# Two heads' scan decays in one place of an image-pair cycle of a gated state-space block

## What is computed

```python
xz = silu(einsum('oc,bchw->bohw', in_proj_w, x) + in_proj_b)
x_ssm, res, gate = split(xz, 3, axis=1)
xf = silu(conv1d(x_ssm, dw_w) + dw_b)
dbc = einsum('oc,bcn->bon', dbc_w, xf) + dbc_b      # per head: dt, B (8 states), C (8 states)
x_h, dt, B_t, C_t = tokens in the order perm[h]       # gathered
dA = exp(softplus(dt) * -exp(A_log));  dB = dt * B_t
h = dA_t * h + dB_t * x_t;  y_t = sum_s h * C_t        # over 1024 tokens, 2 heads, 8 states
y = (y back in image order) * silu(gate) + res
x = x + silu(einsum('oc,bchw->bohw', out_proj_w, y) + out_proj_b)
```

## Time and profile before

| | |
|---|---|
| three runs | 837.87, 838.59 and 839.11 us (median 838.59) |
| the profiled execution | 842.28 us, span from first to last instruction 840.5 us |
| mean granted clock of TensorE | 0.939 of 2.4 GHz |
| busy share of the span | PE 88%, DVE 71%, ACT 61%, POOL 42% |
| chain that ended last | POOL 28%, PE 20%, DMA 19%, DVE 15%, issue 13%, ACT 4% |

### The profile page before, as it was taken

How to read it: one execution, slowest core, us unless ns; L and a number is a source line. 1 busy time by engine, 2 the same in 40 slices (tenths; PEclk the granted TensorE clock), 3 DMA queues, 4 the chain that set the end, 5 groups by cost and what they waited for, 6 DMA issues and landing times.

```text
span 840.5 us, 11680 instructions
## 1 busy us (share of the span) xinstructions
PE 735.4 (88%) x4190; PEld 435.9 (52%) x4190; DVE 592.7 (71%) x1097; ACT 508.6 (61%) x954; POOL 354.4 (42%) x325
## 2 busy tenths in 40 slices
PE   2599867929999999999999999999999999697976
PEld 1356556614566456545755565546654566354642
DVE  5699589624787578957894779577957786378533
ACT  5775745426764875488467756676667764544422
POOL 2295300377038711873087407760577037600330
PEclk9699857969999999999999999999999999998989
DMA  9924550248464937484747564765568434942332
GB/s 329 369 101 165 143 128 1 83 134 212 107 213 144 245 87 246 136 215 120 219 143 189 164 183 156 190 194 131 195 191 213 115 131 142 254 114 87 110 92 100
DMA packets 128539, 136.40 MB, mean 162 GB/s; under 512 B 57305, under 2 KB 107106, under 8 KB 126434
## 3 DMA queue, kind: packets, MB, share of 16 engines
q1 hardware_dynamic: 114448, 99.42, 41.3%
q0 software_dynamic: 12288, 35.80, 13.1%
q10 hardware_dynamic: 1746, 0.45, 0.3%
HBM read 83.08 MB, written 53.61 MB: 163 GB/s over the span
## 4 chain that ended last, share of the span: by engine, by line
POOL 28%; PE 20%; DMA 19%; DVE 15%; issue 13%; ACT 4%; SPq 0%; POOLq 0%; DVEq 0%; ACTq 0%
POOL xt_scratch L462 15%; POOL crow L476 11%; DMA out<-xb 7%; PE pj L1557 7%; PE pj L1429 5%; DMA xb<-in_x 3%; DMA crow<-yt_scratch,idx 3%; DMA xt_scratch<-stage,idx 3%; DVE xf L1040 2%; DVE rs L894 2%; PE tp L1547 2%; POOL xb L443 2%; DMA crow<-cd_scratch 1%; PE tp L1449 1%; DVE xb L1225 1%
## 5 line engine op out<-in xcount | busy, mean ns | idle before, releaser
L1429 PE MATMUL pj<-xb,inw 128*128 128x512 f32 x768 | 350.4, 608 | 21.5 <-POOL xb L443 16.0
L1429 PEld LDWEIGHTS pj<-xb,inw 128*128 128x128 f32 x768 | 144.7, 194 | 187.2 <-issue 155.9
L462 POOL DMA_INDIRECT xt_scratch<-stage,idx x128 | 152.0, 1188 | 80.9 <-issue 73.7
L476 POOL DMA_INDIRECT crow<-yt_scratch,idx x128 | 135.0, 1054 | 109.5 <-DMA yt_scratch<-rs 62.1
L443 POOL TENSOR_SCALAR xb<-xb,pcur 128x1024 f32<-128x1024 f32 x30 | 46.5, 1559 | 257.2 <-DMA xb<-in_x 170.3
L1040 DVE SCALAR_TENSOR_TENSOR xf<-xs,small,xf 128x1024 f32<-128x1024 f32 x64 | 83.9, 1322 | 76.0 <-ACT xf L634 74.5
L1557 PE MATMUL pj<-gt,outw 128*128 128x512 f32 x256 | 118.9, 596 | 0.1
L734 ACT ACTIVATE rs<-pj,small 128x512 f32<-128x512 f32 x64 | 44.2, 694 | 58.1 <-PE pj L1557 58.0
L677 ACT COPY stage<-tp 128x256 f32<-128x256 f32 x128 | 47.8, 374 | 44.9 <-PE tp L1451 42.1
L690 ACT COPY rs<-pj 128x512 f32<-128x512 f32 x64 | 33.0, 600 | 67.7 <-PE pj L1524 67.7
L703 ACT ACTIVATE gt<-pj,pcur 128x512 f32<-128x512 f32 x64 | 41.5, 687 | 46.0 <-PE pj L1429 45.9
(11 more groups left out here) (256 smaller groups left out, 1059.0 us busy)
## 6 DMA issues: line engine op xcount, KB each, us to landing
xb<-in_x SPq DMA_DIRECT2D x16, 1024.0 KB, 5.7
xp<-xt_scratch SPq DMA_DIRECT2D x16, 1024.0 KB, 9.6
crow<-cd_scratch SPq DMA_DIRECT2D x16, 1024.0 KB
out<-xb SPq DMA_DIRECT2D x16, 1024.0 KB, 6.4
yt_scratch<-rs SPq DMA_DIRECT2D x16, 512.0 KB, 3.6
yt_scratch<-rs SPq DMA_DIRECT2D x32, 256.0 KB, 5.4
gt<-in_x SPq DMA_DIRECT2D x4, 1024.0 KB, 12.0
big<-in_x SPq DMA_DIRECT2D x4, 1024.0 KB, 13.7
```

Of the source, the lines that this page charges most:

```text
L462: pool.indirect_dma_start(out=xt_d.ap(), out_offset=bass.IndirectOffsetOnAxis(ap=idx[:, k:k + 1], axis=0), in_=v(stage, (nt * H + h) * ROW ...
L476: pool.indirect_dma_start(out=v(crow, k * NB * P, (1, NB * P)), out_offset=None, in_=yt_d.ap()[0:(h + 1) * N], in_offset=bass.IndirectOffs ...
L1429: last = nc.tensor.matmul(o[:, :], v(inw, ct * 3 * C + col + ot * P, (1, P)), x_view(par, b, ct, nt * HALF, HALF), start=(ct == 0), stop=( ...
```

## The change

`big` now has room for both heads (2 x 8 x 272 columns in place of 8 x 272 and 8 x 256), and the token products are written over the decays they come from, not to a part of their own. ACT's `decays(i+1, 1)` follows `decays(i+1, 0)` directly, ahead of the output units of cycle `i`; `convolved(i+2, 1)` moves from ahead of the decays to behind output unit 3. PE's `segments(i+1, 1)` stands behind output unit 0, ahead of its tile of rows, and waits until head 0's decays are done (`ee_ready`), since `sg` holds one head. `turn_c(i+1, 0)` moves from ahead of unit 4 to ahead of unit 5 and waits for both heads' decays. In the setup, `segments(0, 1)` and `decays(0, 1)` come ahead of `turn_c(0, 0)` on PE and of `convolved(1, 1)` on ACT. On POOL, cycle 0 alone has its scatters ahead of both scalings; from cycle 1 on the order is the old one.

```diff
-        big = sb("big", S * EEW + S * Q * L)
+        big = sb("big", H * S * EEW)
...
             def cycle(i):
+                early = 1 if i else 0
                 if i < PH - 2:
-                    scale_x(i + 2, (0,))
+                    scale_x(i + 2, range(0, early))
                 if i < PH - 1:
                     scatter(i + 1)
                 if i < PH - 2:
-                    scale_x(i + 2, (1,))
+                    scale_x(i + 2, range(early, NB))
...
             def decays(i, h):
-                wait(act, w_ready, i * H + h)
+                wait(act, m_step, (i - 1) * H * 6 + (h + 1) * 6)
...
-                    last = nc.scalar.activation(v(big, s * EEW, (1, EEW)), v(sg, 0, (1, EEW)), ACT.Exp,
+                    last = nc.scalar.activation(v(big, h * HEAD + s * EEW, (1, EEW)), v(sg, 0, (1, EEW)), ACT.Exp,
...
                 if more:
                     rows_out(i + 1, 1)
-                if more:
-                    decays(i, 1)
-                    if not first(i):
-                        gate(i, par, range(0, 4))
-                else:
-                    gate(i, par, range(0, 2))
-                    decays(i, 1)
-                    gate(i, par, range(2, 4))
+                if not first(i):
+                    gate(i, par, range(0, 4))
...
                 residual(i, par, range(2, E_U))
-                if beyond:
-                    convolved(i + 2, 1)
                 if more:
-                    decays(i + 1, 0)
+                    for h in range(H):
+                        decays(i + 1, h)
                 for k in range(O_U):
                     output(i, (k,))
                     if beyond:
                         rows_out(i + 2, 0, (k,))
+                    if beyond and k == O_U // 2 - 1:
+                        convolved(i + 2, 1)
...
             decays(0, 0)
             sigmoid(1)
+            decays(0, 1)
             convolved(1, 1)
...
+                    W = v(big, h * HEAD + SEG + b * NT * L, (EEW, S), (L, NT), (1, L))
                     nc.vector.tensor_tensor(
-                        v(big, W_OFF + b * NT * L, (Q * L, S), (L, NT), (1, L)),
-                        v(big, SEG + b * NT * L, (EEW, S), (L, NT), (1, L)),
+                        W, W,
                         v(crow, h * NT * L * S * NB + b, (NB, S), (S * NB, NT), (NT * S * NB, L)), ALU.mult)
...
             def turn_c(i, h):
                 pe.wait_ge(bc_step, ih * 3 + 3)
+                pe.wait_ge(ee_ready, (i + 1) * H)
+                wait(pe, cblk_ready, ih)
...
                 chunk_sums(i, 0, 0)
-                segments(i, 1)
...
                 for k in range(O_U):
-                    if more and k == 4:
+                    if more and k == 5:
                         turn_c(i + 1, 0)
                     output(i, last, (k,))
+                    if more and k == 0:
+                        segments(i + 1, 1)
                     if beyond:
                         rows(i + 2, 0, (y_drained, (i + 1) * Y_U), (k,))
...
             experts(1)
+            segments(0, 1)
             turn_c(0, 0)
```

More of the change, by code:

```diff
@@ L152, in build @@
         onesb = sb("onesb", 2, mybir.dt.bfloat16)
-        W_OFF = S * EEW
+        HEAD = S * EEW
         HQ = H * Q
@@ L1136, in factors @@
                 nc.vector.tensor_tensor(v(bc8, DBE, (S, Q), (1, S)), v(bc8, DB, (S, Q), (1, S)),
-                                        v(big, SEG + L - 1, (L, Q), (EEW, S)), ALU.mult).then_inc(bc_step, 1)
+                                        v(big, h * HEAD + SEG + L - 1, (L, Q), (EEW, S)), ALU.mult).then_inc(bc_step, 1)
                 wait(dve, c_full, ih)
@@ L1142, in factors @@
                         v(bc8, CS + b * NT * S, (S, NT), (1, S)), v(cn, h * NT * CROW + NB + b, (CROW, NT), (NB, S)),
-                        v(big, CUM + b * NT, (1, NT), (EEW, S)), ALU.mult)
+                        v(big, h * HEAD + CUM + b * NT, (1, NT), (EEW, S)), ALU.mult)
                 last.then_inc(bc_step, 1)
@@ L1179, in token_weights @@
                 dve.wait_ge(w_ready, ih + 1)
-                W = v(big, W_OFF, (Q * L, S), (L, Q), (1, L))
+                of_states = lambda lo, n: v(big, h * HEAD + lo * EEW, (EEW, n), (1, Q * L))
+                W = v(big, h * HEAD, (EEW, S), (L, Q), (1, L))
                 nc.vector.tensor_tensor(W, W, v(bc8, DB, (1, S), (S, Q), (0, L)), ALU.mult).then_inc(m_step, 1)
-                n = S * Q * L
+                n = S
                 for k in (1, 2):
@@ L1185, in token_weights @@
                     dve.wait_ge(m_step, at + 1 + k)
-                    nc.vector.tensor_tensor(v(big, W_OFF, (1, n)), v(big, W_OFF, (1, n)), v(big, W_OFF + n, (1, n)),
-                                            ALU.add).then_inc(m_step, 1)
+                    nc.vector.tensor_tensor(of_states(0, n), of_states(0, n), of_states(n, n), ALU.add).then_inc(m_step, 1)
                 dve.wait_ge(m_step, at + 4)
                 nc.vector.scalar_tensor_tensor(v(m16, 0, (L, Q), (1, L)), const("diag", (0, Q), (1, L)),
-                                               v(small, DPAR + h, (1, 1)), v(big, W_OFF, (L, Q), (1, L)),
+                                               v(small, DPAR + h, (1, 1)), v(big, h * HEAD, (L, Q), (1, L)),
                                                ALU.mult, ALU.add).then_inc(m_step, 1)
                 dve.wait_ge(m_step, at + 5)
-                nc.vector.tensor_tensor(m16[:, :], m16[:, :], v(big, W_OFF + Q * L, (1, Q * L)), ALU.add).then_inc(m_step, 1)
+                nc.vector.tensor_tensor(m16[:, :], m16[:, :], v(big, h * HEAD + EEW, (1, Q * L)), ALU.add).then_inc(m_step, 1)
             def weights_block(i, h):
@@ L1457, in segments @@
                 wait(pe, ee_ready, i * H + h)
-                wait(pe, cblk_ready, i * H + h)
+                wait(pe, cblk_ready, i * H)
                 dt = h * Q
```

## The result

The changed kernel takes 881.06 us (median of four runs, 874.98 to 885.3), against 838.45 us for the kernel before beside it: a ratio of 1.0507, with an interval of 1.0458 to 1.0556. The forecast, slower, was right in its sign; the size was not: 846.7 us was forecast, with a range up to 859. The runs of the changed kernel also lie 10 us apart, where those of the kernel before, beside them, lie 1.2 us apart.

What follows compares the result with a forecast made beforehand. The loop through image 0's store, load of x, scatters and gathers was taken to bound the kernel, PE nearly as tight. Terms -13.7 + 18.0 + 5.0 - 1.2 = +8.1 us gave 846.7 us on the median, range 839.5 to 859.

Steps and rivals of the forecast that it cites:

- The step that failed: Cycle 0 on POOL: scatters start once the biases are added, 134.29 + 0.86, not at 162; net -13.7 us for the cycle.
- The 15.95 goes: Cycle 0: PE's wait of 15.95 us for image 1's scaling disappears, and 2.4 us on the records behind it.
- a rival for a gain that does not come: Another transfer or the gathers hold PE in cycle 0; half the scatters' gain lost gives 856 us; chance 0.06.
- The setup's lateness: Before cycle 0: head 1's sums wait for head 0's decays, so `turn_c` and what follows come 4.7 us late.
- The output stage: PE waits 2.05 us behind unit 0, first drain at S + 10.1, output unit 3 and all behind 5.0 us late.
- The middle: Mid-cycle: sums, loads and decays leave, PE arrives 2.4 us earlier, but DVE's scan lets only 0.8 us come back.
- The rival in which the freed middle counts in full: PE gets back all 2.4 us each cycle, a period grows by 1.8, total 835.3 us; chance 0.10.
- longer by 3.4: Period by PE: 5.0 lost in the output stage, less 0.8 from the middle and 0.8 of the gathers' wait.
- The loop: From S through image 0's store, load of x, scaling, scatters, gathers, `turn_back`: 2.75 to 5.0 us longer, 3.6 taken.
- the +18.0: Five periods, cycles 1 to 5, each longer by the loop's 3.6 us.
- The end: Cycle 6: +5.0 us, its scatters start after cycle 5's outputs; cycle 7: -1.2 us (bounds -4 and +2).
- The clock rival: PE's two output-stage waits lower its clock; sums and two units 2.5 us later, six times: 862 us; chance 0.12.

Runs made afterwards that it cites:

- e2: Kernel before with only POOL's cycle 0 order as the change has it, the wait for the parameters still ahead of the scatters: 843.14 us, ratio 1.0045.
- e4: Changed kernel with POOL's old order in cycle 0, so the decays' part alone: 876.93 us, ratio 1.0419.
- e1: Changed kernel with `scale_x` of an empty range returning before its wait for the parameters: 866.48 us, ratio 1.0333.
- e10: e1 with POOL's wait for the scatters' landing moved behind its gathers: 845.36 us, ratio 1.0083.
- e12: e3 with POOL's wait for the scatters' landing moved behind its gathers: 817.48 us, ratio 0.9748 to the kernel before.
- e3: Kernel before with POOL's new cycle 0 order and no parameter wait in scaling of an empty range: 820.42 us, ratio 0.9782.
- e8: e3 with image 0's load of x put ahead of image 1's store in SP's queue: 824.17 us, ratio 0.9849 to the kernel before.
- e11: Kernel before with separate areas for both heads' decays and weights written over them, every instruction in its old place: 838.67 us, ratio 0.9990.
- e14: Changed kernel with only POOL's wait for the scatters' landing moved behind its gathers: 867.25 us, ratio 1.0337 to the kernel before.
- e9: e1 with image 0's load of x ahead of image 1's store in SP's queue, PE's output-stage waits unfilled: 856.62 us, ratio 1.0206.
- e7: e9 with PE's two output-stage waits filled with output records that the next unit writes over: 852.47 us, ratio 1.0171 to the kernel before.
- e13: e1 with head 1's store of y held in SP's queue until the scatters have landed: 849.37 us, ratio 1.0139 to the kernel before.

## Why the prediction was wrong in size

**The step that failed** is "After: the scatters start when the biases are added, 134.29 + 0.86, not at 162", with all that rests on it: "The 15.95 goes", and the images' scaling at 167.6 and 170. The prediction took the order of POOL's calls for the order of its waits. `scale_x` of an empty range issues its wait for the parameters and nothing else, so the scatters stayed behind it. This part was to give 18.4 us (15.95 and 2.4) and cost about 4 (`e2`, `e4`): S of cycle 0 at +9.2, not -13.7, a miss of 22.9 of the 34.4 us between 846.7 and 881.1. The text had a rival for a gain that does not come, but priced half of it lost, and named transfers and gathers as the cause. That a moved wait stays in place was not on the list. With the wait taken out (`e1`) the paragraph held from its start to its end: the first scatter at 140.3 where 141 was written, S at 202.7 where 216.34 - 13.7 is 202.6. That close it came by luck: from `e4` to `e1` S moves by 19.0 us for the 18.4, and the setup costs 5.3 for 4.7, two misses of 0.6 that cancel. The scatters took 26.9 us, not 23.4, and the cover that the prediction had counted held that.

**The setup's lateness** was right: `turn_c` and what follows 4.7 us later were forecast; DVE waits 4.73 us for it, and S of cycle 0 in `e4` is 5.3 us later than before.

**The output stage** was right: the wait (2.05 forecast, 2.09), the first drain (S + 10.1, S + 10.4), the third tile's wait, and the units behind it (5.0 us later forecast, 5.2).

**The middle** was right in its mechanism, and a little too small: PE then waits 0.66 to 0.92 us ahead of head 1's `within`, for DVE's weights (the profile names an ACT gate in some cycles, but PE starts 0.14 to 0.15 us behind the weights in all), and 0.3 us ahead of `carry`, for DVE's scan. In the period of 90.9 us that starts at 502.73, the last output unit is 5.2 us later after S than before, head 1's `from_states` 3.9 us: 1.3 came back (0.8 forecast, 2.4 at the most). The rival in which the freed middle counts in full did not come. Where PE does not wait for the gathers, the change's period is 90.9 us, 2.9 longer than before, where "longer by 3.4" was written.

**The loop** was mis-sized twice. First the load of x. It goes out at S + 25.8 (25.4 forecast), 0.4 us behind image 1's store. Image 0's x takes 7.1 to 7.9 us to land, where "2 MB at 368 GB/s take 5.7 us" was written, and scaling starts at S + 33.1 to 33.9, not S + 31.7. Image 1's load, which those 2 MB (the store and image 0's load) leave out, is in flight too from S + 30.3 on. The sum has a slip as well: 25.4 and 5.7 make 31.1, not 31.7, and by 31.1 the loop is 3.0 longer and not the 3.6 that the +18.0 is made of. The stretch while x lands, in cycle 0 (busy times as above, then clock, DMA share, GB/s), is at the rate that the prediction used, for longer:

```profile
252.00:259.50 7.50, 7.49 (x47) 5.32 (x46) 7.22 (x14) 3.68 (x15) 0.10 (x1) 1.00 1.01 364
```

Second, from there the loop has two outcomes, as the rows above show, and the forecast has one. The step that it lacks is POOL's wait for the scatters' landing. That wait was in the trace of before, 1.7 us a cycle; the prediction did not ask what its length hangs on. Where the landing is on time, the gathers start 2 us later after S than before, PE is not held by them, and a period grows by 2.8 to 3.0 us; where it is late, by 4.6, 5.2 and 8.1, the last with the clock's part. These make the +23.7 for the 18.0 forecast, so 3.6 is the size of none of them. That five periods of `e10` are 18.7 us longer than those of `e12` (455.5 against 436.8) does not confirm the 18.0: in both PE doesn't wait for the gathers, so the loop of the forecast binds in neither.

**The end.** Cycle 6 added 2.2 (5.0 forecast) and the last cycle gave 2.5 (1.2 forecast). Cycle 6 is 85.5 to 90.7 us long in the ten kernels with the change's decays, so the 5.0 is neither borne out nor refuted. The last cycle of the profiled execution of before, 79.2 us, is long among its kind (79.5 in `e2`, but 74.2 to 75.4 in `e3`, `e8`, `e11` and `e12`). What the last cycle won was won against a long one.

**The sum** of these, against the forecast, is 22.9 for cycle 0, 5.7 for the periods, -2.8 and -1.3 for the end: 24.5. Another 9.9 us lies between executions: the profiled one of before was 3.8 over the median measured beside the change, that of the change 6.1 under its own. No trace shows the other executions. That the landing makes most of their difference is argued from `e14`, where four of five runs agree within 2 us; some of it may be in every kernel, since the runs of the kernel before beside all the experiments went from 834.4 to 842.6.

**The clock rival** came in its mechanism and not in its price. With the two waits, the granted clock of `e9`'s output stages is 0.59 to 0.79, but that costs from nothing to 1.6 us a cycle, since a wait behind the unit had the time; 2.5 was written. It also falls where the rival did not look, behind PE's wait for the gathers (1.5 us in the period of 96.1). The Trainium skill (TensorE: Matmul & The Clock Gate, "Loop structure matters more than you think") says that waits between bursts of matmuls leave the array cold; the stages of `e9` and `e7` agree, 0.59 with the waits and 1.00 without. The row of a wait of 2.05 us, on which the prediction set that rule aside, was half a guide: in the change's six output stages with the same waits the second unit is slow in two.

## What to carry to other kernels

When a call is made empty in order to move it, look at the waits it issues outside its loop: an order of calls is not an order of waits, and one look at the first instruction behind the moved place settles it. A wait for a transfer that nothing on its own engine needs at that point belongs as late as its reader allows; here it turned 1.2 us into 4. And a load that goes out right behind a store is priced with all that is in flight until it lands: here it took 7.1 us and more, where the same load took 5.0 to 5.4 before.

## What was not expected of the hardware

An indirect DMA's issue on POOL takes 0.96 us alone, and 3.67 us where it meets DVE's pair of products, each with both inputs in SBUF:

```profile
358.55 3.81 DVE L1169 TENSOR_TENSOR big<-big,crow 128x1024 f32<-128x1024 f32 x2
...
449.43 3.84 DVE L1169 TENSOR_TENSOR big<-big,crow 128x1024 f32<-128x1024 f32 x2
```

The scatters at 359.57 and 450.45 both start 1.02 us into such a pair. The first took 1.76 us and the next slipped in behind it; the second took 3.67. Why one found the gap between the two products and the other did not is open, and in these two cycles it decided between a period of 91 and one of 93. The Trainium skill (SBUF — State Buffer, "Who interferes with whom") says that a DVE instruction with two SBUF inputs and a GpSimd one that reads SBUF exclude each other. These rows agree with it, if the issue of an indirect DMA counts as such a reader, which no run here shows.

A plain store from SP made scatters from POOL land late, though different engines issue them. In the changed kernel's chain of waits the last scatter of cycle 1, issued with the store of y, took over 5 us to land:

```profile
285.36 5.34 DMA xt_scratch<-stage,idx
```

In `e13`, with that store held back, the last one of cycle 3 had landed by 447.54, at most 3.8 us after its issue began at 443.74.
